# Scan operands loaded two steps ahead, and row stores in larger, earlier pieces: a graph layer followed by a two-way ConvLSTM on one core

## The reference, cut to what matters

```
def step(carry, xr):                       # xr: one row, 16 images x 48 channels x 32 columns
    h, c = carry
    inp = concatenate([xr, h], axis=1)     # 96 channels
    gates = conv1d(inp, w_mid) + b         # 3 taps along the row, 192 outputs
    i, f, g, o = split(gates, 4)
    c2 = sigmoid(f) * c + sigmoid(i) * tanh(g)
    h2 = sigmoid(o) * tanh(c2)
    return (h2, c2), h2
```

## Time and profile before

| what | value |
|---|---|
| median of three runs | 644.28 us |
| the profiled execution's own time | 645.12 us |
| its span in the profile | 643.1 us |
| PE busy in the span | 548.7 us (85%) |
| DVE busy | 510.8 us (79%) |
| ACT busy | 445.2 us (69%) |
| POOL busy | 257.7 us (40%) |
| chain that ended last | DVE 24%, PE 20%, transfers 20%, SP's queue 15%, issue 11%, ACT 6% |

### The profile page before, as it was taken

The page is one execution under the profiler, slowest core; times in us unless marked ns, Lnnn a source line. Parts: engine busy times, 40 slices in busy tenths (PEclk is TensorE's granted clock), DMA queues, the critical chain, the costliest instruction groups (busy, mean ns, idle before and its releaser), DMA issues.

```text
span 643.1 us, 11780 instructions
## 1 busy us (share of the span) xinstructions
PE 548.7 (85%) x3160; PEld 335.2 (52%) x3160; DVE 510.8 (79%) x1091; ACT 445.2 (69%) x709; POOL 257.7 (40%) x361
## 2 busy tenths in 40 slices
PE   6992699999999978889878988999997998989870
PEld 1232466666666645556545555666664655555530
DVE  2686769999999998889997867777887665777765
ACT  3771369999999988879875756676775655666545
POOL 2650004333333322224844745455555343445400
PEclk9996689999999999989997999999999988999985
DMA  8847655566667878877753355444445444443416
GB/s 212 264 143 208 198 118 141 140 141 140 143 143 175 182 173 195 180 151 155 175 127 63 94 139 140 128 135 139 130 136 150 122 128 129 129 135 119 125 52 196
DMA packets 112519, 94.74 MB, mean 147 GB/s; under 512 B 54560, under 2 KB 86818, under 8 KB 112146
## 3 DMA queue, kind: packets, MB, share of 16 engines
q1 hardware_dynamic: 111714, 90.64, 55.1%
q10 hardware_dynamic: 768, 3.67, 2.3%
HBM read 65.61 MB, written 26.48 MB: 143 GB/s over the span
## 4 chain that ended last, share of the span: by engine, by line
DVE 24%; PE 20%; DMA 20%; SPq 15%; issue 11%; ACT 6%; POOL 2%; DVEq 1%; ACTq 0%; POOLq 0%
DVE hmax L1276 6%; DMA hp<-hist_d 6%; DMA ht<-xl_d 5%; DMA idx_d<-idx 4%; PE pz L741 3%; DVE onehot L1261 3%; PE pz L583 3%; DVE cu L1374 3%; PE pz L749 3%; DVE idx L1252 2%; SPq L429 2%; SPq L338 2%; PE pz L661 2%; PE p_edge L741 2%; ACT cu L940 2%
## 5 line engine op out<-in xcount | busy, mean ns | idle before, releaser
L1276 DVE TENSOR_REDUCE hmax<-gel 96x128 f32<-96x1024 f32 x128 | 151.8, 1204 | 10.2 <-ACT gel L874 10.1
L874 ACT ACTIVATE gel<-pz 96x1024 f32<-96x1024 f32 x128 | 130.5, 1019 | 29.2 <-PE pz L661 18.4
L1159 POOL CAST xh<-h 48x256 fp32r<-48x256 f32 x124 | 53.8, 459 | 126.4 <-DVE h L1396 124.0
L940 ACT ACTIVATE cu<-c 48x256 f32<-48x256 f32 x128 | 48.4, 414 | 53.6 <-DVE c L1387 53.6
L749 PE MATMUL pz<-ht,w_rows 128*112 128x512 f32 x258 | 71.0, 412 | 5.7 <-DMA ht<-xl_d 5.7
L1161 POOL TENSOR_TENSOR ht<-h,xh 48x512 fp32r<-48x512 f32 x62 | 73.5, 1185 | 5.0
L741 PE MATMUL pz<-xh,w_rows 128*112 128x512 f32 x258 | 73.3, 421 | 1.8 <-POOL xh L1159 1.4
L661 PE MATMUL pz<-onehot,ab_hi 64*96 64x512 f32 x256 | 59.9, 464 | 4.6 <-ACT gel L874 4.0
L1396 DVE SCALAR_TENSOR_TENSOR h<-tgo,cu 48x256 f32<-48x256 f32 x128 | 50.0, 430 | 14.6 <-ACT cu L940 9.4
L741 PEld LDWEIGHTS pz<-xh,w_rows 128*112 128x112 f32 x258 | 45.2, 182 | 27.8 <-POOL xh L1159 9.0
L749 PEld LDWEIGHTS pz<-ht,w_rows 128*112 128x112 f32 x258 | 45.1, 181 | 27.3 <-DMA ht<-xl_d 12.6
(11 more groups left out here) (145 smaller groups left out, 1124.9 us busy)
## 6 DMA issues: line engine op xcount, KB each, us to landing
ib<-idx_d SPq DMA_DIRECT2D x64, 256.0 KB, 4.5
xt<-xl_d SPq DMA_DIRECT2D x64, 197.6 KB
y_d<-y SPq DMA_DIRECT2D x32, 192.0 KB, 3.4
y_hl<-y_d SPq DMA_DIRECT2D x32, 192.0 KB, 3.8
hist_d<-h SPq DMA_DIRECT2D x62, 96.0 KB, 5.2
hp<-hist_d SPq DMA_DIRECT2D x30, 192.0 KB, 3.3
ht<-xl_d SPq DMA_DIRECT2D x128, 33.1 KB, 2.9
xl_d<-xh SPq DMA_DIRECT2D x16, 198.4 KB, 3.4
```

The source lines that it names most:

```text
L874: act.activation(gel[:, t % 2], pz[0:O, 2 * (t % 2):2 * (t % 2) + 2, :], ACT.Gelu) \
L940: act.activation(to, c, ACT.Tanh, scale=0.5).then_inc(S["tanh_c"], 1)
L1159: pool.tensor_copy(head[:, BX * n:BX * n + BX], columns(h)).then_inc(S["h_top"], 1)
L1276: dve.tensor_reduce(dst, gel[:, t % 2].rearrange("p w (r c k) -> p w r c k", r=WS, k=KN), AX_X, ALU.max).then_inc(S["maxed"], 1)
```

## The change: what it does

`ht` gets a second buffer per direction, chosen by the step's parity, with a semaphore for each buffer. In a step of the scan SP loads the thirds of s+2 in place of s+1, at the place in its list where it loaded those of s+1; the first two steps' thirds are loaded in turns 28 and 29. `load_h(s-1)` moves from the end of the step to the middle, behind the `store_h` of direction 0. `store_lows` and `load_twins` take four rows a call and go to other places: rows 0 to 7 are stored in turns 10 and 11 and twinned in 12 and 13, rows 24 to 31 are stored in 18 and 19 and twinned in 20 and 21, rows 16 to 23 are stored in 26 and 27 and twinned in 30 and 31, rows 8 to 15 go in steps 2 and 3 (store in the half of direction 0, twins in that of direction 1). The scan weights move to turns 8 to 15, the tap weights to 16 to 20, the small constants to 21 to 25. SP's instructions are written out from turn 8 on.

```
-        ht = sb("ht", [P, 2, SLOT], F32R)
+        ht = sb("ht", [P, 2, 2, SLOT], F32R)
...
             def store_lows(r, sem):
...
-                    sp.dma_start(xl_d[r:r + 2, first:first + rows].rearrange("r c n -> c r n"),
-                                 xh[src:src + rows, r:r + 2, 0:SLOT - 1].bitcast(F32)).then_inc(S[sem], 16)
+                    sp.dma_start(xl_d[r:r + 4, first:first + rows].rearrange("r c n -> c r n"),
+                                 xh[src:src + rows, r:r + 4, 0:SLOT - 1].bitcast(F32)).then_inc(S[sem], 16)
...
             def load_thirds(s, d):
 
                 for q in range(2):
-                    sp.dma_start(ht[HALF * q + C:HALF * q + HALF, d, 0:SLOT - 1].bitcast(F32),
-                                 xl_d[row_of(s, d), 32 + 16 * q:C + 16 * q]).then_inc(S[f"x_third{d}"], 16)
+                    sp.dma_start(ht[HALF * q + C:HALF * q + HALF, d, s % 2, 0:SLOT - 1].bitcast(F32),
+                                 xl_d[row_of(s, d), 32 + 16 * q:C + 16 * q]).then_inc(S[f"x_third{d}{s % 2}"], 16)
...
-                    load_shifts(0, d)
-                    load_thirds(0, d)
-                    load_shifts(1, d)
+                    for s in range(2):
+                        load_shifts(s, d)
+                        load_thirds(s, d)
...
                 if isinstance(j, int) and j > 0:
...
+                    if 8 <= g < 16:
+                        load_scan_weight(g - 8)
+                    elif 16 <= g < 21:
+                        load_tap_weight(g - 16)
+                    elif 21 <= g < 26:
+                        load_rest(g - 21)
+                    for first, r, n in ((10, 0, 0), (18, 24, 0), (26, 16, 1)):
+                        if first <= g < first + 2:
+                            sp.wait_ge(S["x1_split"], first - 2)
+                            store_lows(r + 4 * (g - first), f"xl_stored{n}")
+                        elif g in (first + 2, first + 3) and n == 0 or g >= 30 and n == 1:
+                            load_twins(r + 4 * (g % 2), f"x_twins{n}")
...
             def step(s):
                 for d in range(2):
-                    if s + 1 < H:
+                    if s + 2 < H:
                         sp.wait_ge(S["gates"], s * 4 + (2 * d + 2))
-                        load_thirds(s + 1, d)
-                    if s + 2 < H:
+                        load_thirds(s + 2, d)
                         load_shifts(s + 2, d)
                     store_h(s, d)
+                    if s >= H // 2 + 1 and d == 0:
+                        load_h(s - 1, 1 - s % 2)
                     if 6 <= s < H // 2 + 6:
                         load_x1r(s - 6, d)
-                    if 2 <= s < 6:
-                        (store_lows, load_twins)[d](4 + 2 * s, ("xl_stored1", "x_twins1")[d])
-                if s >= H // 2 + 1:
-                    load_h(s - 1, 1 - s % 2)
+                    if 2 <= s < 4:
+                        (store_lows, load_twins)[d](4 * s, ("xl_stored1", "x_twins1")[d])
```

More of the change, by code:

```diff
@@ L249, in by_row, with h_slots @@
             return t.rearrange("c (r w) -> c r w", w=W)
-        def h_slots(t, first, d):
-            return t[first:first + C, d, 1:1 + (W + 1) * B].rearrange("p (b w) -> p b w", w=W + 1)[:, :, 0:W]
+        def h_slots(first, d, b):
+            return ht[first:first + C, d, b, 1:1 + (W + 1) * B].rearrange("p (b w) -> p b w", w=W + 1)[:, :, 0:W]
         def column_halves(t):
@@ L428, in load_twins @@
                 for first, src in ((C, HALF), (TOP, HALF + 16)):
-                    sp.dma_start(xh[first:first + 16, r:r + 2, 0:SLOT - 1].bitcast(F32),
-                                 xh[src:src + 16, r:r + 2, 0:SLOT - 1].bitcast(F32)).then_inc(S[sem], 16)
+                    sp.dma_start(xh[first:first + 16, r:r + 4, 0:SLOT - 1].bitcast(F32),
+                                 xh[src:src + 16, r:r + 4, 0:SLOT - 1].bitcast(F32)).then_inc(S[sem], 16)
             def load_shifts(s, d):
@@ L458, in turn @@
                 if isinstance(j, int) and j > 0:
[L459 to L460 removed]
+                    g = nth(j, b, 0)[0]
+                    if g == 8:
                         sp.wait_ge(S["rests_set"], 1)
                         sp.wait_ge(S["xn_stored3"], 32 * (CHUNKS // 2 + 1))
[L463 to L479 removed]
+                    if 8 <= g < 16:
[10 more added lines that the diff above has]
+                            load_twins(r + 4 * (g % 2), f"x_twins{n}")
             load_y(3, 1, 1)
@@ L483, in _ @@
                 turn(0, b)
-            with sp.Fori(1, GROUPS // 2 - 9) as j:
+            with sp.Fori(1, 4) as j:
                 for b in range(2):
                     turn(j, b)
-            for j in range(GROUPS // 2 - 9, GROUPS // 2):
+            for j in range(4, GROUPS // 2):
                 for b in range(2):
@@ L543, in _ @@
                 step(s)
-            sp.wait_ge(S["xl_stored1"], 32 * 8)
+            sp.wait_ge(S["xl_stored1"], 32 * 4)
             for b in range(2):
@@ L742, in h_part @@
                                   start=False, stop=False)
-                pe.wait_ge(S[f"x_third{d}"], s * 32 + 32)
+                pe.wait_ge(S[f"x_third{d}{s % 2}"], s // 2 * 32 + 32)
                 if later(s):
@@ L749, in h_part @@
                         mm = pe.matmul(gate_banks(k, d)[m][0:TOP, :], w_rows[:, 1, d, m, t],
-                                       by_column(ht[:, d, t:t + (W + 1) * B]), start=False, stop=(t == TAPS - 1))
+                                       by_column(ht[:, d, s % 2, t:t + (W + 1) * B]), start=False, stop=(t == TAPS - 1))
                     mm.then_inc(S["gates"], 1)
@@ L777, in _ @@
             pe.wait_ge(S["first_rows"], 2)
-            pe.wait_ge(S["x_twins0"], 32 * 8)
+            pe.wait_ge(S["x_twins0"], 32 * 4)
             pe.wait_ge(S["wl_split"], 3)
@@ L790, in _ @@
                 step(s, s)
-            pe.wait_ge(S["x_twins1"], 32 * 8)
+            pe.wait_ge(S["x_twins1"], 32 * 4)
             for s in range(8, 14):
@@ L940, in tanh_cell, with h_edge @@
                     act.activation(to, c, ACT.Tanh, scale=0.5).then_inc(S["tanh_c"], 1)
-            def h_edge(s, d):
+            def h_edge(s, d, b):
                 act.wait_ge(S["h2_ready"], s * 4 + (2 * d + 2))
-                act.activation(h_slots(ht, HALF, d), h2[0:C, d].rearrange("p (b w) -> p b w", w=W), ACT.Copy) \
+                act.activation(h_slots(HALF, d, b), h2[0:C, d].rearrange("p (b w) -> p b w", w=W), ACT.Copy) \
                     .then_inc(S["h_edge"], 1)
@@ L953, in step @@
                 for d in range(2):
-                    prev = (s - 1, 1) if d == 0 else (s, 0)
+                    prev = (s - 1, 1, k % 2) if d == 0 else (s, 0, (k + 1) % 2)
                     more = later(s) if d == 0 else not isinstance(s, int) or s + 1 < H
@@ L1083, in first_rows @@
             def first_rows():
-                pool.wait_ge(S["xl_stored0"], 32 * 8)
+                pool.wait_ge(S["xl_stored0"], 32 * 4)
                 for n, row in enumerate((0, H - 1)):
@@ L1180, in _ @@
                 if s == 7:
-                    pool.wait_ge(S["xl_stored1"], 32 * 8)
+                    pool.wait_ge(S["xl_stored1"], 32 * 4)
                 for d in range(2):
```

25 lines of the change are left out of this document (3 added, 22 removed).

## The result

Four runs of the changed kernel took 622.69, 622.89, 628.08 and 628.15 us, median 625.49; the kernel before had a median of 644.29 beside it. The ratio is 0.970 with the interval 0.964 to 0.976. The execution that was profiled is one of the two short ones, 622.89 us, with a span of 621.1 us; against the profile of before (645.12 and 643.1) it is 22.2 us shorter. The forecast was 618 in a range of 610 to 630: the direction and the range held, the sum of the gains was about 4 us too large in the profile and 7 us in the medians.

A forecast was written before the change was run, and what follows sets the result against it. DVE bounds the turns until SP is late in 18 to 24; PE and its waits bound the scan. 8.9 + 1.4 + 3.0 + 13.3 - 0.5 = 26.1 us off 645.12 leaves 619.0, as a median 618, range 610 to 630.

The forecast's parts named there:

- the 7.33 us of an early step and the 8.39 of a late one: Scan: 7.33 us taken as PE's floor without the projection, 8.39 as a step with it that no load holds up.
- Turns 14 to 24: Turns: moving or halving SP's issues ends its lag, so the stretch of turns 18 to 24 goes, 8.9 us gained.
- the 5.1 that had cost nothing: Turns 14 to 17 before the change: SP fell 5.1 us behind over four turns without costing DVE anything.
- The 0.5 set against crowding: Turns 10 to 13: loss of 0.5 us, between 0 and 4, for extra traffic that comes earlier.
- Rival B: Turns 10 to 21: larger pieces crowd the transfers, DVE loses there what it gained in 18 to 24; 626.6 us, chance 0.10.
- Turns 28 to 31: End of the turns: SP's result store goes out earlier, ending DVE's wait in turn 31; gain 1.4 us, bounds 0 and 1.7.
- Thirds two steps ahead: Early scan, steps 4 to 9: the wait for `ht` goes; gain 3.0 us, bounds 0 and 5.2.
- h loaded mid-step: Late scan, steps 19 to 31: an earlier load of h removes PE's waits; gain 13.3 us, bounds 7.4 and 15.9.
- The charge of four steps at 9.04 and nine at 8.39: Late scan: four steps with residual rows charged at SP's loop of 9.04 us, should the landing grow to 6; costs 2.6 us.
- rival C: Scan: SP's new wait holds back the stores of h; slower from a landing of 7.6 us, 650 us at 8; chance 0.04.
- A: Scan: the transfers set the step, late scan gains about 7 us and early scan nothing; 627.5 us, chance 0.16.
- D: Late scan: the wait for `hp` isn't shortened, late gain only 7 to 8 us; near 624 us, chance 0.08.

The follow-up runs named there:

- xt_three: The changed kernel with the load of `xt` made as three transfers of 32 channels, one for each shift: 617.95 us, ratio 0.955.
- thirds_only: The kernel before with only the second buffer of `ht` and the thirds loaded two steps ahead: 640.58 us, ratio 0.989.
- turns_only: The kernel before with only the change's four-row pieces, weights and constants at their new places: 645.93 us, ratio 1.000.
- loadh_only: The kernel before with only the load of h moved to the middle of the step: 635.98 us, ratio 0.984.
- pieces_behind_index: The changed kernel with the turns' row stores and twins issued right behind the index store of the same turn: 623.18 us, ratio 0.964.
- h2_two_buffers: The changed kernel with two buffers of h2 per direction, so DVE waits for the store of two steps ago: 633.59 us, ratio 0.982.

## Why the prediction came out as it did

*What bounds the kernel.* Right: SP was the pacer of turns 18 to 24, and the stored h that of the late scan. Each of the two parts that were aimed at a wait took that wait away when it was made alone. Two numbers were read as floors and are none: the 7.33 us of an early step and the 8.39 of a late one still hold the slow load of `xt`. In xt_three most steps from 6 to 18 take 7.0 us and those from 22 on 8.0.

*Turns 14 to 24, the term that was mis-sized most: forecast -8.9 + 0.5, measured -4.6 in all turns, of which turn 31 is 1.35.* The working said that a four-row piece is as quick to issue as a two-row piece, and it is (0.92 us). The step that failed is the next sentence: 7.8 us of issues in turns 10 and 11. It counted only the piece's own issue; the issue behind it took 2 us more, and the index stores behind the pieces took 5.2, 5.7 and 4.8 us. From one index store's issue to the next SP took 8.82, 11.06, 7.64 and 10.54 us from 164.76 on, 38.1 in all where DVE's pace is 4 x 7.96 = 31.8: a lag of 6.2 us, above the 5.1 that had cost nothing. Of it 4.7 us came out in turns 14 and 16. The 3.4 of turn 14 came out through PE, its late keys and then its clock, a path that the prediction doesn't have. The 0.5 set against crowding, with 4 as its bound, came out at 8.9 - (4.6 - 1.35) = 5.6 in this profile. The reason for the low value was that 5.1 us of lag had cost nothing; but that lag was spread over four turns of SP's issuing, and here the index store itself was late. Rival B had the mechanism, and its sign, a turn of 10 to 21 above 8.5 us, came. The share of 0.81 that it leaned on says little, since turns at 0.83 (200 to 290 us) ran at 8.09 us: a mean over 90 us hides the six-microsecond stretches at 1.04 and 1.07 beside the late index stores. What kind of traffic stretches a turn is settled this far: not the form of a piece (two runs) and not the weights alone (one run). That it is the sum that SP sends in these turns fits all of them but isn't shown by itself. What holds up SP's issue behind a piece no view shows, and it stays open.

*Turns 28 to 31: forecast -1.4, measured 8.70 - 7.35 = -1.35.* Right: DVE's timeline lists no wait in turn 31, and that turn takes 7.0 to 7.5 us in every kernel with the new places of the pieces, 8.70 and 8.71 in the two without. Another 1.6 us between turn 31 and the first h2 were not forecast.

*Thirds two steps ahead: forecast -3.0, measured -0.2 in steps 3 to 9.* The mechanism and size were right by themselves (-3.0 in thirds_only). The clause that failed is that rows 8 to 15 going in two steps and not four would cost half a microsecond: turns_only has steps 3 to 9 2.3 us longer than before, with PE waiting for `ht` in steps 4 and 5, and the whole change loses there what the thirds gain. With the thirds early it is the stores of h that are late: the prediction had noted the 1.73 us wait of step 3 and left it where it was, and it became five waits of 1.1 to 2.6 us in steps 3 to 5.

*h loaded mid-step: forecast -13.3, measured -13.8.* Right, and alone responsible (111.1 us with and without the rest). The charge of four steps at 9.04 and nine at 8.39 makes 111.7 us; the trace has four at 9.21 and nine at 8.25. The premise was a landing that grows from 5.2 to 6, and it grew to 6.2. That the sum fits so closely is in part luck: in loadh_only the landing is 5.3 us, PE waits for `ht`, and the stretch is as long. And the gain beyond the 13.3 us of waits was put down to the chain behind PE; the trace has the clock there, with PE's 4.5 us of busy time. Two sub-forecasts were off. SP waits 2.4 and not 0.7 us ahead of the load (0.9 in loadh_only), and PE and its weight loads still wait up to 1.0 and 1.9 us for `hp`, where none above 0.5 was forecast. Neither is the pacer: DVE is, waiting for the store of h, as rival C described its loop but at a landing of 6.2, below its deciding 7.6.

*The rivals.* The times of A, B and D (627.5, 626.6 and near 624) all lie nearer to the median than the forecast. D did not hold: the late scan gained 13.8 us and not 7 to 8. B took 5.6 of its 8.9 us. The parts of A did not come true: the late scan gained in full. Its mechanism is in the kernel all the same, as the reason for the slow landings: the load of `xt`, three packets at a time. The reading against it, that the transfer engines are busy only 0.44 of the stretch, was the wrong measure: a mean is low when one transfer keeps only a few packets in flight for most of the time. In xt_three, whose stores land 4.2 us earlier, that mean is higher, 0.53 in the same stretch against 0.42 in the change.

*Sum.* In the profile 4.6 + 1.6 + 0.5 + 0.2 + 0.7 + 13.8 + 0.6 = 22.0 us of the 22.1, against 26.1 forecast: the turns are short by 5.2 (9.8 forecast with turn 31), the thirds by 2.8, the late scan over by 0.5, and 3.4 came from stretches with no term. That the result lies in the range is luck in part: 8.0 us of the forecast did not come, and 3.4 came from where nothing was forecast. The median lies another 2.6 us above the profiled execution; the two longer runs were not profiled, so where they lose 5 us isn't known.

## What to carry to other kernels

When many small transfers land late while the mean share of the transfer engines is low, look for one transfer with a short slowest dimension (the outermost one, of 3 for `xt`) among them and cut it so that every piece has many rows, before rearranging waits; then measure, since the same kind of cut brought nothing for `kr`. Price a moved transfer by what is issued behind it and by the landing of the next small one, not by its own issue. When two parts of a change use the same stretch (thirds and rows 8 to 15 here), cost them there together: one took back what the other gave. Look at the granted clock of PE before pricing a wait of PE: four waits here cost more than their own length.

## What the runs showed of the hardware

- A pair of stores of 397 and 132 KB is issued in 0.92 us, but the next two issues, of 48 KB each, take 3.05 instead of 0.88 us (in pieces_behind_index the stores of x1, of the same size, take 2.94 instead of 1.02); as four stores of half the size the hold-up falls inside the four issues (2.81 us).
- With one load of three times 32 rows a 96 KB store of h lands after 6.2 us, with three loads of 32 rows after 2.0, with 128 transfers more to issue and a shorter kernel (ratio 0.955 against 0.970). The packets of the one load are mostly three at a time, those of the three loads mostly eight or more.
- Taking away a wait for a slow landing made that landing slower (6.2 to 7.3 us in h2_two_buffers) and did not shorten the kernel (0.982 against 0.970, overlapping intervals).
- An 8 KB index store takes 5.2 to 5.7 us while the transfer share is 1.04 to 1.07, and leads to the next issue after 2.8 us in a quieter turn.
- After waits of PE of 1.7 to 3.1 us its granted clock was 0.50 (1.2 GHz) for a while: four times in the late scan of before, 13.7 us in all, and from 191.8 to 198.7 us in the changed kernel.
